# The attention block's layer norm computed one sample ahead, its root and its scaling at other steps, and the output projection one step later

## The reference, cut to what matters

```
emb   = silu(sin_emb(timestep)) @ W_ada + b_ada        # scale and shift per sample
h     = layernorm(x) * (1 + scale) + shift             # no learned weights in this norm
q,k,v = h @ Wq + bq, h @ Wk + bk, h @ Wv + bv          # 16 heads of 16
score = q k^T / sqrt(16) + attention_bias              # bias: 8 x 16 x 512 x 512 f32, read once
score = where(mask, -inf, score);  p = softmax(score)
x1    = h + (p @ v) @ Wo + bo
```

## Time and profile before

| | |
|---|---|
| median of 3 runs | 1039.86 us |
| span of the profiled execution, first to last instruction (the profile gives no other time of its own for it) | 1036.6 us |
| PE busy | 92% |
| DVE, ACT, POOL busy | 78%, 71%, 70% |
| mean granted TensorE clock | 0.986 |
| start of step 0 of samples 0, 1, 2, 3, 4 (first transpose of the step) | 41.28, 125.05, 209.07, 293.07, 377.04 us |

### The profile page before, as it was taken

One profiled execution on the slowest core, in us unless ns is written; L12 is line 12 of the kernel. 1 busy time (PEld: TensorE's weight loads), 2 busy tenths in 40 slices (PEclk: granted clock), 3 DMA queues, 4 the chain that ended last, 5 costly groups with the idle time before them and its releaser, 6 DMA issues. The chain is left out here.

```text
span 1036.6 us, 20438 instructions
## 1 busy us (share of the span) xinstructions
PE 956.1 (92%) x5892; PEld 640.9 (62%) x5892; DVE 813.7 (78%) x2075; ACT 734.7 (71%) x1211; POOL 726.3 (70%) x596
## 2 busy tenths in 40 slices
PE   5879999999999999999999999898999999999963
PEld 4646556656655655755665665454777777777752
DVE  8887797878879879879787887874456877887697
ACT  3577887888798788788788878875446556655433
POOL 3487697788788878878778878777555567755631
PEclk9989999999999999999999999999999999999987
DMA  7978978997996997897799799752111111111001
GB/s 262 334 289 292 381 289 278 363 347 238 346 384 214 336 386 257 291 390 292 265 372 343 237 348 370 252 193 82 41 41 41 42 33 50 42 41 41 21 21 41
DMA packets 127535, 230.33 MB, mean 222 GB/s; under 512 B 5488, under 2 KB 53872, under 8 KB 123632
## 3 DMA queue, kind: packets, MB, share of 16 engines
q1 hardware_dynamic: 127472, 229.60, 62.0%
HBM read 187.63 MB, written 41.94 MB: 221 GB/s over the span
## 5 line engine op out<-in xcount | busy, mean ns | idle before, releaser
L937 ACT ACTIVATE prob<-prob,nmax 128x512 f32<-128x512 f32 x512 | 357.0, 729 | 59.6 <-DVE nmax L762 56.4
L762 DVE CUSTOM_DVE_ANT_0 prob<-s_bank,big 128x512 f32<-128x512 f32 x512 | 338.7, 684 | 69.7 <-POOL big L1101 40.3
L1101 POOL TENSOR_TENSOR big<-big,mterm_early 128x2048 f32<-128x2048 f32 (+2 forms) x88 | 305.3, 3484 | 71.5 <-DMA big<-in_fside_Bx16xSxS 62.3
L593 PEld LDWEIGHTS t_bank<-ident,prob 128*128 128x128 f32 x2048 | 238.1, 141 | 168.3 <-issue 51.5
L593 PE MATMUL t_bank<-ident,prob 128*128 128x128 f32 x2048 | 317.7, 278 | 15.9 <-ACT prob L937 6.7
L944 ACT COPY pt<-t_bank 128x512 f32<-128x512 f32 x312 | 181.1, 584 | 51.7 <-PE t_bank L593 50.6
L581 PE MATMUL s_bank<-stack_k,stack_q 128*128 128x512 bf16 x512 | 195.4, 382 | 1.3 <-DVE nmax L762 0.7
L771 DVE COPY pt<-t_bank 128x512 f32<-128x512 f32 x200 | 137.2, 686 | 34.9 <-PE t_bank L593 34.6
L2052 POOL TENSOR_TENSOR gl<-big,gh 128x512 fp32r<-128x512 f32 x64 | 84.6, 1329 | 69.8 <-DVE gh L1643 69.8
L607 PE MATMUL o_bank<-pt,val 128*32 128x512 f32 x1024 | 122.9, 598 | 1.2 <-ACT pt L944 0.7
L1905 ACT ACTIVATE big<-bank,late 128x512 f32<-128x512 f32 x62 | 42.7, 689 | 75.2 <-PE bank L1446 71.4
(11 more groups left out here) (257 smaller groups left out, 1610.0 us busy)
## 6 DMA issues: line engine op xcount, KB each, us to landing
big<-in_fside_Bx16xSxS SPq DMA_DIRECT2D x128, 1024.0 KB, 8.0
pieces_dram<-pieces SPq DMA_DIRECT2D x64, 384.0 KB, 7.3
stack_q<-pieces_dram SPq DMA_DIRECT2D x15, 1024.0 KB, 8.3
stack_k<-pieces_dram SPq DMA_DIRECT2D x15, 1024.0 KB, 10.0
pieces_dram<-pieces SPq DMA_DIRECT2D x32, 256.0 KB, 7.6
xin<-in_x SPq DMA_DIRECT2D x8, 512.0 KB, 8.7
x_dram<-x SPq DMA_DIRECT2D x8, 512.0 KB, 2.6
x1r<-x_dram SPq DMA_DIRECT2D x8, 512.0 KB, 4.3
```

Source lines behind the costliest of these rows:

```text
L593: last = pe.transpose(t_bank[n % 2][:, c * P:(c + 1) * P], prob[:, n % NT, c * P:(c + 1) * P], ident[:])
L762: dve.tensor_tensor_reduce(out=prob[:, n % NT, :], in0=s_bank[n % 3][:, :], in1=bias[:, h % NB, t, :], scale=-1.0, scalar=3e38, op0=ALU.ad ...
L937: act.activation(tile, tile, ACT.Exp, bias=nmax[:, n % NT:n % NT + 1], scale=-1.0).then_inc(exped.sem, 1)
L1101: pool.tensor_tensor(bias[:, h % NB, tiles], bias[:, h % NB, tiles], mterm[:, tiles], ALU.add).then_inc(masked.sem, 1)
```

## The change

Per sample, the norm of sample b+2 is now prepared within iteration b: x of b+2 is loaded at head 6; its statistics are taken one tile a step at steps 44 to 47, aggregated at 48, where VectorE also adds eps (one new small `tensor_scalar`); ScalarE takes the root at step 53, VectorE normalises one tile a step at 58 to 61. Iteration 0 does this also for its own next sample, at steps 3, 5 and 8 to 11. TensorE's transposes XT move from steps 14, 15 to 15, 16, its W uses from 10, 12 to 11, 13 (each has two parts, one a step), GpSimd's residual from 15 to 16. The sqrt reads std in place instead of mv with a bias. Iteration 6 is written out for SyncE and ScalarE. The semaphores of `apart` are merged into one.

```diff
-HEADS_OF_LOADS = dict(x1=3, first=2, ...)
-STATISTICS_AT, DEVIATION_AT, NORMALISE_AT = 11, 12, 14
-RESIDUAL_AT = 15
-TAIL = [("O", 3, 6, 1), ("C", 0, 7, 1), ("C", 1, 9, 1), ("W", 0, 10, 1), ("W", 1, 12, 1)]
-AHEAD = [("XT", 0, 14, 0), ("XT", 1, 15, 0), ("Q", 0, 21, 0), ...]
+HEADS_OF_LOADS = dict(x=6, x1=3, first=2, ...)
+STATISTICS_AT, AGGREGATE_AT, ROOT_AT, NORMALISE_AT = (44, 45, 46, 47), 48, 53, (58, 59, 60, 61)
+FIRST_STATISTICS_AT, FIRST_ROOT_AT, FIRST_NORMALISE_AT = 3, 5, (8, 9, 10, 11)
+RESIDUAL_AT = 16
+TAIL = [("O", 3, 6, 1), ("C", 0, 7, 1), ("C", 1, 9, 1), ("W", 0, 11, 1), ("W", 1, 13, 1)]
+AHEAD = [("XT", 0, 15, 0), ("XT", 1, 16, 0), ("Q", 0, 21, 0), ...]
...
 # SyncE, iteration
-                if not last and not first:
-                    load_x(b)
+                    if h == HEADS_OF_LOADS["x"] and not last and not before_last:
+                        load_x(b + 1)
...
 # VectorE
+            def aggregate(b, counted):
+                link(counted)
                 for t in range(QT):
                     last = dve.bn_aggr(mv[:, t], stats[:, t])
+                    link(last)
+                    dve.tensor_scalar(std[:], mv[:, :, 1], EPS, None, ALU.add).then_inc(shifted.sem, 1)
...
+            def normalise_tile(b, t):
+                if t == 0:
+                    dve.wait_ge(root_done.sem, root_done.at(b, 1))
+                    link(dve.reciprocal(rstd[:], std[:]))
+                done = dve.tensor_scalar(xin[:, t], xin[:, t], mv[:, t, 0:1], rstd[:, t:t + 1], ALU.subtract, ALU.mult)
...
+                ahead = b + 1 < B - 1
-                    if not last and n == STATISTICS_AT:
-                        statistics(b)
-                    if not last and n == NORMALISE_AT:
-                        normalise(b)
+                    if ahead and n in STATISTICS_AT:
+                        counted = statistics_of(b + 1, STATISTICS_AT.index(n))
+                    if ahead and n == AGGREGATE_AT:
+                        aggregate(b + 1, counted)
+                    if ahead and n in NORMALISE_AT:
+                        normalise_tile(b + 1, NORMALISE_AT.index(n))
...
 # ScalarE, after take_turned and before take_context of the same step
+            def root(b):
+                act.wait_ge(shifted.sem, shifted.at(b, 1))
+                act.activation(std[:], std[:], ACT.Sqrt).then_inc(root_done.sem, 1)
+                    if n == ROOT_AT and not last and not before_last:
+                        root(b + 1)
```

More of the change, by code:

```diff
@@ L537, in _ @@
             iteration(0, first=True)
-            with sp.Fori(1, B - 1) as b:
+            with sp.Fori(1, B - 2) as b:
                 iteration(b)
+            iteration(B - 2, before_last=True)
             iteration(B - 1, last=True)
@@ L772, in take_turned, with statistics_of @@
                                 t_bank[n % 2][:, :].rearrange("p (c q) -> p c q", c=QT)).then_inc(evac[1].sem, 1)
[L774 to L778, removed]
+            def statistics_of(b, t):
+                if t == 0:
+                    dve.wait_ge(x_in.sem, x_in.at(b, 16))
+                return dve.bn_stats(stats[:, t], xin[:, t])
+            def aggregate(b, counted):
+                link(counted)
                 for t in range(QT):
                     last = dve.bn_aggr(mv[:, t], stats[:, t])
-                last.then_inc(stat_done.sem, 1)
+                if b < 0:
+                    last.then_inc(stat_done, 1)
+                else:
+                    link(last)
+                    dve.tensor_scalar(std[:], mv[:, :, 1], EPS, None, ALU.add).then_inc(shifted.sem, 1)
             def first_statistics(s, b, i):
@@ L855, in iteration @@
                         take_turned(b, n - 1)
-                    if not last and n == STATISTICS_AT:
-                        statistics(b)
-                    if not last and n == NORMALISE_AT:
-                        normalise(b)
+                    if first and n == FIRST_STATISTICS_AT:
+                        for t in range(QT):
+                            counted = statistics_of(b, t)
+                        aggregate(b, counted)
+                    if first and n in FIRST_NORMALISE_AT:
+                        normalise_tile(b, FIRST_NORMALISE_AT.index(n))
+                    if ahead and n in STATISTICS_AT:
[4 more added lines that the diff above has]
+                        normalise_tile(b + 1, NORMALISE_AT.index(n))
                     if last and n == NORMALISE_LAST:
@@ L898, in _ @@
             setup["angles"](dve)
-            statistics(-1)
+            for t in range(QT):
+                counted = statistics_of(-1, t)
+            aggregate(-1, counted)
             setup["domains"](dve)
@@ L993, in iteration @@
                         take_turned(b, n - 1)
-                    if n == (DEVIATION_LAST if last else DEVIATION_AT):
+                    if n == FIRST_ROOT_AT and first:
+                        root(b)
+                    if n == ROOT_AT and not last and not before_last:
+                        root(b + 1)
+                    if last and n == DEVIATION_LAST:
                         deviation(b)
@@ L1062, in copy_values @@
                     pool.wait_ge(weighed.sem, weighed.at(b, g + 1))
-                apart(pool, pool_apart)
+                apart(pool, k["apart"])
                 for t in range(QT):
@@ L1700, in statistics @@
                 wait(dve, bn_done[i], j, 1)
-                apart(dve, dve_apart)
+                apart(dve, k["apart"])
                 for t in range(QT):
@@ L2160, in build @@
             k[n] = nc.alloc_sbuf_tensor_at(n, [P] + shape, dt, offset=at)
-        for n in ("first_in", "w1_made", "w2_made", "x1_last", "first_made", "mix_step"):
+        for n in ("first_in", "w1_made", "w2_made", "x1_last", "first_made", "mix_step", "apart"):
             k[n] = ctx.enter_context(nc.semaphore(n))
```

71 lines of the change are left out of this document (35 added, 36 removed).

## The result

The changed kernel took 1120.42 us (median of 4 runs, 1119.22 to 1122.61) against 1039.98 us before (median of 4, 1038.04 to 1041.15): ratio 1.0772, interval 1.0753 to 1.0791. The prediction was 1085, range 1052 to 1104: slower was right, and the time lies 16 us above the range. The profiled execution has a span of 1117.4 us, 80.8 more than before.

What follows compares the result with a forecast made beforehand. TensorE, busy 92% of the span, was taken as the bound. A + B + C + D = 0.6 + 2.9 + 3.2 + 1.0 = 7.7 us, six times, with E 0 and F -0.8, gave +45.4: 1085 us, range 1052 to 1104.

Steps and rivals of the forecast that it cites:

- the steps that would pay: TensorE's waits at steps 10 to 14, where the norm is: 2.4 us a sample, all the change can win.
- the sign: Whole kernel: slower, given a chance of 0.90; same 0.03, faster 0.07.
- C: Norms at steps 58 to 61: the fourth is held by the mask of h1, 3.2 us a sample; alternatives 1.0 and 5.3.
- walk: VectorE's operations timed one by one from tile 57's copy: fourth norm at 378.5, mask of h1 starting between 377.4 and 378.0.
- A: Statistics on VectorE at steps 44 to 48 delay the add of step 48: 0.6 us a sample, bounds 0 and 1.4.
- D: Lower clock after the waits of root and norms: 1.0 us a sample, bounds 0 and 1.95.
- E: Steps 10 to 22, samples 1 to 6: 2.4 us gained, residual behind h6's mask; net 0, bounds -2.4 and +1.1.
- rival 3: At step 48 the eps add is blocked behind a GpSimd mask too: 1094 us, chance 0.10.
- B: ScalarE's root at step 53 with two table loads, read from a trace row: 2.9 us a sample, bounds 0.3 and 2.9.
- F: The ends: sample 0 net 0, bounds -3 and +3; sample 7 gains 0.8 us.
- Rivals 1 and 2: 1: no norm meets h1's mask, 1069 us, chance 0.20; 2: residual in time, 1071 us, chance 0.12.
- Rival 4: Late delays are absorbed in the next sample's steps 0 to 4: faster, 1025 us, chance 0.07.

Runs made afterwards that it cites:

- experiment 5: Changed kernel with the next sample's x loaded at head 4 instead of head 6: 1109.97 us, ratio 1.0641 to the kernel before.
- Experiment 6: Changed kernel with only the root moved, from step 53 to 50: 1090.66 us, ratio 1.0474 to the kernel before.
- experiment 12: Changed kernel with statistics at 30 to 33, root 34, norms 51, x's load at head 4, W and XT at their old steps: 1036.70 us, ratio 0.9964.
- experiments 7 to 12: Changed kernel with root, norms and x's load (from 8 on also statistics) at other steps: 1047.68, 1039.31, 1037.76, 1039.01, 1037.62, 1036.70 us.
- experiment 4: Kernel before with only W, XT and the residual moved a step later, norm as before: 1051.74 us, ratio 1.0111.

## Why the prediction was wrong

The bound, the steps that would pay and the sign were right, but the sum of 7.7 a sample was 13.4. More than half of the miss is in C, whose walk had the mask's start wrong; A left out a wait, D one of two stretches at the lower clock, and E put the residual's cost too low.

- *A*, 0.6, measured 1.7 (44 to 47). The statistics' own part is 0.92 (0.27 + 0.65, experiment 5). The other 0.8 is a term that the prediction didn't have: it followed where x's load leaves the queue, at the sample's start (in E), and not what it stands ahead of at head 6. The eps add took 0.53 us beside a mask (306.50 to 307.03; the mask to 307.01) and 0.17 in sample 5 where no mask ran. So rival 3's mechanism is right, with a price of 0.36, hidden: steps 48 to 50 are as long as before. Rival 3's ground against it, the reciprocal of the same size, didn't carry over from one operation to the other. The Trainium skill's page "SBUF — State Buffer", section "Who interferes with whom", states that a `tensor_scalar` in a two-port mode and a GpSimd op lock each other out for the whole instruction; the rows of eps add and norms agree, and the reciprocal, which it doesn't list there, keeps its 0.17.
- *B*, 2.9, measured 2.9. The row decided rightly: 1.28 each way and 0.20 of sqrt, and step 54 is 2.91 longer in each of samples 0 to 5. The Trainium skill's page "ScalarE: Activation LUTs", section "What ACT_TABLE_LOAD costs", has 2.66 us a switch; this trace does not agree, and the measurement decides. That it would be split over O 2 and T55 was right too.
- *C*, 3.2, measured 6.3: the failed step is "it starts between 377.4 and 378.0", the start of h1's mask. It took from the kernel before that this mask starts 9.7 us after its load is issued (367.74 to 377.44). In the changed kernel the issue doesn't wait for the root, and the load lands sooner. DMA time to landing, before (h1 and h2 in sample 3) and after (h1 in sample 2, the shortest of six):

```profile
DMA to landing us min/median/max: 9.4/9.4/9.5
```

```profile
DMA to landing us min/median/max: 7.3/7.3/7.3
```

Over samples 0 to 5 h1's load lands in 9.5 to 10.2 us before and in 7.3 to 9.2 after; the mask starts 7.5 us after the issue in sample 2 (313.51 to 321.01) and 8.4 to 9.4 in the others. Counted from T53, the walk had the first norm at 8.6 us and the mask at 10.4 to 11.0. Measured are 8.5 to 9.9 for the norm and 8.3 to 10.2 for the mask. The mask is early in all six. In samples 0 and 4 the norm stands where the walk had it; in the other four it is about 1 us late, by the lower clock at steps 55 and 56 (D). So the norms meet the mask with the first or second and not the fourth, and a later one meets the mask of h2 as well, which the walk didn't follow. Experiment 6 shows the walk's order, but partly by luck: there the mask starts 8.0 to 9.0 us after its load's issue and the fourth norm 9.2 to 9.4, where the walk had 9.7 and 10.2 to 10.8, so both are early.
- *D*, 1.0, measured about 0.8 at steps 55 and 56 and 1.4 at 61 and 62, 2.2: in samples 1, 2, 3 and 5 each of the two waits was followed by a stretch at the lower level, in 0 and 4 only the second; the prediction had one for both.
- *E*, net 0, measured +0.6: the gains are 2.7 (forecast 2.4), the residual costs 3.3 (forecast 2.4). Counted from step 0, the xth cast came 0.8 to 1.1 later than before, as forecast. But the prediction priced only the wait of Q at step 21. TensorE lost its time earlier: 2.1 us at step 18, where it waits for the adds behind VectorE's copy of XT 0, and 1.15 at step 20, where it waits for a copy that stands behind the cast on ScalarE. The mask terms did start nearer to the sample's start (17.9 us after step 0 in sample 2, 19.2 before), which the prediction had hoped for from x's absence. In experiment 12, where x's load is moved too, they start at 19.2 on average against 19.5, so x's absence by itself isn't what brought it.
- *F*, sample 0 net 0 in its first half, measured about +2.1: inside its bounds, though a norm of 4.1 us met a mask.

Summed: A 1.1, C 3.1, D 1.2 and E 0.6 more, less 0.3 in small steps, are 5.7 a sample; six times 5.7 and sample 0's 2 make 36, against 35 between 1085 and 1120. The errors were not independent. Each delay moved the next instruction towards or deeper into a mask, and the mask itself came sooner; C's bounds took its start as nearly fixed. What made the loads land sooner stays open (see the last section). Rivals 1 and 2 needed what did not happen. Rival 4's absorption didn't come: steps 0 to 4 are as long as before.

## What to carry to other kernels

A `tensor_scalar` of VectorE that starts during one of GpSimd's mask additions ends with it (0.40 us become up to 4.2). Its price is what is left of the mask when it is issued, so place it in a gap of both engines, and work out that place with all other delays of the change in; here the masks start when loads land, and these landed at another time too. A moved load must be followed in both directions: what gets free where it was and what it delays where it goes. The root, which costs 2.9 us at step 53, cost 0.5 to 0.9 three steps earlier, beside a long group of matmuls.

## What was not expected of the hardware

- Bias loads landed in a median of 8.0 us before and 6.9 after, the same 1 MB from the same queue. Slowness alone isn't the reason: in experiments 7 to 12, whose profiled spans are within 0.4% of the kernel before, the median is 7.0 to 7.3, and in experiment 4, slower but with x's load in its old place, it is 8.0. For h1's load it is not x's place alone either: 9.5 to 10.2 us before, 7.3 to 9.2 after, 8.7 to 9.6 in experiment 5 (nearly as slow as the changed kernel) and 9.1 to 9.8 in 12. The cause stays open.
- A mask holds even a `tensor_scalar` of 128x4 elements (the eps add: 0.53 instead of 0.17 us, and 1.71 in sample 2 of experiment 5), while a bn_stats that starts during a mask (301.52, mask from 300.84) takes its 0.42 as ever.
- TensorE's waits of 1.30 and 1.42 us ahead of O 2 and of T55 (1.17 and 1.51 in sample 0) stand in every one of samples 0 to 5, in the changed kernel and in experiment 5. In samples 1, 2, 3 and 5 of the changed kernel transposes at the lower level of 1.2 GHz follow (1.06 instead of 0.66 us), in samples 0 and 4, and in all samples of experiment 5, the clock stays at 2.4 GHz there. What decides between the two isn't shown.
